# A decoder on one core: the maximum pass of cross attention in four tiles, and newer self attention and last experts

## The reference

```python
x = x + L0_attn(layernorm(x))                     # 16 heads of 64
x = x + L0_xattn(ctx_1024, layernorm(x))          # ("context mixing")
x = x + L0_ffn(layernorm(x));  x = x + L1_attn(layernorm(x))
x = x + L1_xattn(layernorm(x), ctx_1024, ctx_1024)    # the same in layers 2 and 3
# cross attention of layers 1 to 3, 16 heads of 8:
#   Q, K, V = projections;  scores = Q K^T * scale
#   attn = softmax(scores);  out = (attn V) Wo + bo
...
x = x + L3_ffn(layernorm(x))
# 32 experts take at most 70 tokens each, 16 adapters shared by pairs:
#   idx = argsort(-score)[:cap];  out = scatter_add(w * expert(x[idx]))
```

## Time and profile before

| what | us |
|---|---|
| median of three runs (4217.76 to 4238.39) | 4232.51 |
| the profiled execution | 4240.81 |
| its span, first to last instruction | 4239.0 |
| PE busy | 3631.5 (86%) |
| DVE busy | 2559.1 (60%) |
| ACT busy | 2099.3 (50%) |
| POOL busy | 1553.1 (37%) |
| mean granted clock of TensorE | 0.929 |

### The profile page before, as it was taken

How to read it: one execution, slowest core, us unless ns; L and a number is a source line. 1 busy time by engine, 2 the same in 40 slices (tenths; PEclk the granted TensorE clock), 3 DMA queues, 4 the chain that set the end, 5 groups by cost and what they waited for, 6 DMA issues and landing times. The chain is left out here.

```text
span 4239.0 us, 113125 instructions
## 1 busy us (share of the span) xinstructions
PE 3631.5 (86%) x48174; PEld 2493.0 (59%) x48174; DVE 2559.1 (60%) x4447; ACT 2099.3 (50%) x2832; POOL 1553.1 (37%) x1827
## 2 busy tenths in 40 slices
PE   7976459999997887799999988978899999983698
PEld 5654227777775445477777754434477777761475
DVE  4522568877774445578777753345578777756543
ACT  3344437766664232267666652344376666651010
POOL 1100037667661000267667620012476676620000
PEclk9998779999998899999999988988899999995798
DMA  4062045655651430356655621100356556520575
GB/s 147 2 252 104 2 108 148 151 145 147 156 140 37 97 85 4 93 140 151 154 141 149 156 50 55 54 7 8 85 138 155 149 140 159 150 57 1 141 194 130
DMA packets 203247, 464.39 MB, mean 110 GB/s; under 512 B 87486, under 2 KB 94398, under 8 KB 202590
## 3 DMA queue, kind: packets, MB, share of 16 engines
q1 hardware_dynamic: 200622, 455.30, 41.4%
q10 hardware_dynamic: 2160, 2.29, 0.2%
HBM read 212.72 MB, written 1.72 MB: 51 GB/s over the span
## 5 line engine op out<-in xcount | busy, mean ns | idle before, releaser
L1435 DVE TENSOR_REDUCE x_bank_top<-ps 112x1 f32<-112x500 f32 x2304 | 1419.2, 672 | 469.8 <-PE ps L1151 463.3
L1287 ACT ACTIVATE x_probs_t<-ps 128x1344 f32<-128x1344 f32 x768 | 991.8, 1291 | 211.3 <-PE ps L1168 206.8
L1168 PEld LDWEIGHTS ps<-x_queries,x_keys 128*128 128x128 bf16 x9216 | 488.1, 98 | 330.4 <-issue 150.3
L1151 PE MATMUL ps<-x_keys,x_queries 96*112 96x500 bf16 x2304 | 633.8, 381 | 24.7 <-DMA x_keys<-x_key_part 15.2
L1168 PE MATMUL ps<-x_queries,x_keys 128*128 128x112 bf16 x9216 | 584.2, 213 | 38.8 <-ACT x_probs_t L1287 36.6
L1181 PE MATMUL ps<-x_probs_t,x_values 128*32 128x112 f32 x18432 | 490.5, 263 | 5.5 <-ACT x_probs_t L1287 4.1
L1181 PEld LDWEIGHTS ps<-x_probs_t,x_values 128*32 128x32 f32 x18432 | 443.3, 111 | 70.2 <-issue 65.2
L1368 POOL TENSOR_TENSOR x_key_part<-x_key_whole,x_nothing 128x500 bf16<-128x500 f32 x270 | 337.2, 1249 | 255.9 <-ACT x_key_whole L1272 255.9
L1372 POOL TENSOR_TENSOR x_key_part<-x_key_left,x_nothing 128x500 bf16<-128x500 f32 x270 | 340.4, 1261 | 21.2
L1139 PE MATMUL ps<-x_wv,x_ctx_t 128*128 128x128 f32 (+1 forms) x2304 | 329.3, 286 | 10.4 <-issue 10.4
L1151 PEld LDWEIGHTS ps<-x_keys,x_queries 96*112 96x112 bf16 x2304 | 258.9, 131 | 128.0 <-DVE x_bank_top L1435 37.1
(11 more groups left out here) (455 smaller groups left out, 4521.8 us busy)
## 6 DMA issues: line engine op xcount, KB each, us to landing
x_keys<-x_key_part SPq DMA_DIRECT2D x1143, 192.0 KB, 3.7
x_ctx_t<-in_ctx_t SPq DMA_DIRECT2D x96, 750.0 KB, 6.1
cm_ctx_n<-in_ctx_n SPq DMA_DIRECT2D x32, 768.0 KB, 6.0
cm_ctx_t<-in_ctx_t SPq DMA_DIRECT2D x32, 750.0 KB, 8.3
e_share<-m_weight_scratch SPq DMA_DIRECT2D x32, 490.0 KB
e_spread_out<-m_slot_scratch SPq DMA_DIRECT2D x32, 490.0 KB
x_queries<-x_query_part SPq DMA_DIRECT2D x558, 28.0 KB, 2.7
e_share<-m_weight_rows SPq DMA_DIRECT2D x32, 448.0 KB, 6.1
```

The source lines that it names most:

```text
L1151: nc.tensor.matmul(ps[0:RW, n, 0:KB], queries[i // 2 % 2][0:TALL, p, i % 2, :], keys[i % 2][0:TALL, p, KB * n:KB * n + KB], start=True, st ...
L1168: mm = nc.tensor.matmul(ps[:, TURNED + c // VC, RW * (c % VC):RW * (c % VC) + RW], keys[i % 2][:, p, KT * c:KT * c + KT], queries[i // 2 % ...
L1287: nc.scalar.activation(probs_t[PROBS[p]].rearrange("k (n c) r -> k n (c r)", c=VC), ps[:, TURNED:TURNED + VR, 0:VC * RW], ACT.Exp, scale=s ...
L1435: nc.vector.tensor_reduce(bank_top[0:RW, p, n:n + 1], ps[0:RW, n, 0:KB], AX_X, ALU.max).then_inc(topped, 1)
```

## The change

In cross attention the maximum pass goes by single heads. The slots lie in the rows 16 to 111, so that each head of a pair lies in one half of the 128 rows; a call does four matmuls of 64 rows and 64 columns, for two pairs (column halves) and two heads (row halves), into two banks: 12 calls an item in place of 24 matmuls. The rows for the maxima are now 0 to 15 and 112 to 127; ACT alone places the maxima, and POOL clears them again for a later item. A call stands before and one after values or keys in a step, and one between two halves of each mix. Self attention normalises inside its block, has three load semaphores, two mix buffers, and makes its scores two pairs ahead, behind the mix. The last experts have a ring of three buffers, no loops, loads of rows ahead of weights, and gather from three bf16 parts of the tokens, which ACT and POOL split beside the router.

```diff
@@ self_attention_0
+        norm = Norm(chip, x, xn, True, squares, roots, (4, 5, 6, 7))
...
-            for n in range(-1, NP_):
+            for n in range(-2, NP_):
                 if n >= 0:
                     turn(n)
-                if n + 1 < NP_:
-                    make_scores(n + 1)
-                if n > 0 and n % 2 == 0:
-                    project_out(n // 2 - 1)
                 for g, t in halves(n):
                     project(g, t)
                 if n >= 0:
                     mix_values(n)
-                if n + 1 < NP_:
+                if n + 2 < NP_:
+                    make_scores(n + 2)
+                if 0 <= n + 1 < NP_:
                     make_values(n + 1)
+                if n > 0 and n % 2 == 0:
+                    project_out(n // 2 - 1)
...
         @block.scalar
...
                 for g, t in halves(n):
                     if t % 4 < 2:
                         keep_made(g, t)
-                if n + 1 < NP_:
-                    exponentials(n + 1)
+                if 0 <= n + 1 < NP_:
                     keep_values(n + 1)
+                if n + 2 < NP_:
+                    exponentials(n + 2)
...
@@ cross_attention
-            def scores(i, p):
...
-                for n in range(NB_):
-                    wait(pe, topped, NB_ * (PR * i + p - 1) + n + 1)
-                    nc.tensor.matmul(ps[0:RW, n, 0:KB], queries[i // 2 % 2][0:TALL, p, i % 2, :], keys[i % 2][0:TALL, p, KB * n:KB * n + KB],
-                                     start=True, stop=True).then_inc(scores_done, 1)
+            def scores(i, m, n):
...
+                unit = UNITS * (HP_ * i + m) + 2 * n
+                for c in range(2):
+                    for r in range(2):
+                        if c == 0:
+                            wait(pe, topped, unit + r - 2)
+                        p, rows = 2 * m + c, slice(64 * r, 64 * r + 64)
+                        mm = nc.tensor.matmul(ps[64 * c:64 * c + 64, (unit + r) % NB_, 0:KB], queries[i // 2 % 2][rows, p, i % 2, r, :],
+                                              keys[i % 2][rows, p, KB * n:KB * n + KB], start=True, stop=True)
+                        if c == 1:
+                            mm.then_inc(scores_done, 1)
...
             def turn_tops(i, h):
...
-                nc.tensor.matmul(ps[TALL:P, MIX, 2 * RW:3 * RW], top_parts[:], ident_low[:, 0:RW], start=True, stop=True).then_inc(tops_turned, 1)
+                for r in range(2):
+                    mm = nc.tensor.matmul(ps[0:TOPS, MIX, 2 * RW + P * r:2 * RW + P * r + P], top_parts[:, r, :], ident_low[:], start=True, stop=True)
+                mm.then_inc(tops_turned, 1)
...
+                    ahead, pair = divmod(step + LEAD, PR)
+                    if has(i + ahead) and pair % 2 == 0 and step % HP_ != 1:
+                        scores(i + ahead, pair // 2, 0)
                     if step in VALUE_STEPS and has(i + 1):
                         make_values(i + 1, VALUE_STEPS.index(step))
                     if step == FOLD_STEP and has(i - 1):
                         fold(i - 1)
-                    ahead, pair = divmod(step + LEAD, PR)
-                    if has(i + ahead):
-                        scores(i + ahead, pair)
+                    if has(i + ahead) and pair % 2 == 1:
+                        scores(i + ahead, pair // 2, 2)
                     if step in KEY_STEPS and has(i + 3):
                         make_keys(i + 3, KEY_STEPS.index(step))
-                    if step == 0 and has(i - 1):
-                        mix_values(i - 1, 1)
-                    if step == HP_ and has(i):
-                        mix_values(i, 0)
+                    if has(i + ahead) and pair % 2 == 0:
+                        scores(i + ahead, pair // 2, 1)
+                    for part in range(2):
+                        if step == 0 and has(i - 1):
+                            mix_values(i - 1, 1, part)
+                        if step == HP_ and has(i):
+                            mix_values(i, 0, part)
+                        if step % HP_ == 0 and part == 0:
+                            ahead, pair = divmod(step + 1 + LEAD, PR)
+                            if has(i + ahead):
+                                scores(i + ahead, pair // 2, 0)
...
+            def place_tops(i, h):
+                act.wait_ge(tops_turned, 2 * i + h + 1)
+                for r in range(2):
+                    turned = ps[0:TOPS, MIX, 2 * RW + P * r:2 * RW + P * r + P].rearrange("k (c s) -> k c s", c=2)[:, :, 0:S]
+                    last_copy = nc.scalar.copy(of_batch(i)[0:TOPS, HP_ * h:HP_ * h + HP_, r].rearrange("k (m c) s -> k m c s", c=2), spread(turned, 1, 2))
+                last_copy.then_inc(tops_placed, 1)
...
                     if has(i):
                         exponentials(i, step)
+                    if step == 2 and has(i):
+                        place_tops(i, 1)
+                    if step == 6 and has(i + 1):
+                        place_tops(i + 1, 0)
...
+            for part in query_parts:
+                nc.gpsimd.memset(part[:, :, :, S:], 0.0).then_inc(zeros_ready, 1)
...
-                    nc.vector.tensor_reduce(bank_top[0:RW, p, n:n + 1], ps[0:RW, n, 0:KB], AX_X, ALU.max).then_inc(topped, 1)
...
+                    nc.vector.tensor_reduce(bank_top[:, m, r, n:n + 1], ps[:, unit % NB_, 0:KB], AX_X, ALU.max).then_inc(topped, 1)
...
@@ experts_by_slot
-    PAIRS, SUBS, LOADS = 16, 2, 6
+    PAIRS, SUBS, LOADS, DEEP = 16, 2, 6, 3
...
+            for n in range(PAIRS):
+                u = n % DEEP
+                if n >= DEEP:
+                    sp.wait_ge(used[u], n // DEEP)
...
-                    mm = nc.tensor.matmul(ps[:, gather_bank(u), 0:2 * CAP], by_token[:, t, :], marks[u][:, t].rearrange("p e k -> p (e k)"),
-                                          start=(t == 0), stop=(t == NP_ - 1))
+                    for k in range(PARTS):
+                        mm = nc.tensor.matmul(ps[:, gather_bank(n), 0:2 * CAP], token_parts[k][:, t, :], marks[n % 2][:, t].rearrange("p e k -> p (e k)"),
+                                              start=(t == 0 and k == 0), stop=(t == NP_ - 1 and k == PARTS - 1))
```

323 lines of the change are left out of this document (183 added, 140 removed).

## The result

The change makes the kernel slower by half a per cent. Median of 19 runs 4257.24 us (4229.74 to 4309.42) against 4236.43 us for the kernel before (19 runs, 4217.76 to 4245.44); ratio 1.0051, 95% interval 1.0036 to 1.0066, so +15 to +28 us. I had forecast 4192, -40 us. The time lies inside the range, but the sign is wrong.

A forecast was written before the change was run, and what follows sets the result against it. PE was taken as the bound of the cross attentions, the bulk of the time. Cross attention +14 and +4, self attention -18 and experts -40 summed to -40 us against the median 4232.5: 4192, range 4115 to 4275.

The forecast's parts named there:

- The steady pass: Cross attention, one pass on PE from one L1157 to the next: 22.45 us, against 22.29 before.
- the terms of a quad: Cross attention: four small matmuls at once take 0.23 us with their starts; each change of tile shape 0.13.
- My own stretches, 13.6 and 8.87: Parts of a cross-attention pass: 13.6 us from L1168 of step 5 to L1157, set by POOL; 8.87 the rest, PE's own.
- POOL's wait ahead of L1214: End of a pass's first stretch: PE would still wait there for POOL, whose chain takes 13.6 us against PE's 13.5.
- At each stage's start ... 1.5 x 3 = +4 us: Cross-attention stage starts: POOL clears three more pads, 0.5 us each, and ACT waits; +4 us over three stages.
- +0.15, times 96: Cross attention: each of 96 passes grows by 0.15 us, +14 us in all.
- My slower rival: Cross attention: shape changes cost more, 0.8 us a pass, +80 us, 4270; slower from +0.6 a pass; chance 0.17.
- Its 4390: Severe form of the slower case: row halves do not overlap, a quad takes 0.43 us, +2 us a pass.
- Self attention: forecast -18: Earlier weight loads -8.7 us, scores two ahead 3 of 11 us kept and 6 at the end; between -12 and -26.
- "Their rate is bounded by that 13.2 us": Last experts: with three buffers loads run without a gap, 13.2 us a set; steps of 13.6, -32 us over 15.
- the third rival: Little gain: loads hold experts at 14.5 us a step, self attention gives only its head; 4214 to 4225; chance 0.2.
- The 8 us for the last step: Last experts: the last step's 3.17 us on DVE's path and the low clock go, -8 us.

The follow-up runs named there:

- rows_split: Kernel before, each load of 32 rows into partitions 96 to 127 issued as two of 16 neighbouring partitions; ratio 1.0051 (1.0031 to 1.0071), +22 us.
- rows_strided: Kernel before, each load of 32 rows issued as two of 16, the even and the odd partitions of 96 to 127; ratio 0.9996 (0.9975 to 1.0016).
- changed_again: The changed kernel unaltered, run and profiled once more on another chip; ratio to the kernel before 1.0073 (1.0047 to 1.0099).

## Why the prediction was wrong

- The steady pass was right: 22.43 us against 22.45, in both stretches, and with it the terms of a quad: 0.21 us for itself (I had 0.23 with its starts) and 0.09 to 0.13 for a change of shape. (My own stretches, 13.6 and 8.87, add up to 22.47; the slip is 2 us in the whole.) One reading of it was not: POOL's wait ahead of L1214 is gone. PE's own first stretch is 13.65 us where I had 13.5, and POOL is done with the maxima 0.18 us before it ends.
- "At each stage's start ... 1.5 x 3 = +4 us" failed, and it is the step that turned the sign. The pads cost nothing that can be seen. The loads of the pair rows, which the diff splits and moves, delay the first fill by 12 us a stage, 35 in all, and I had priced them at nothing without giving a reason. I had looked at the passes and not at the start of a stage. rows_split and rows_strided show the cause of 7 of the 12: sixteen neighbouring partitions a load where there were thirty-two.
- "+0.15, times 96" took every pass as steady. Of the 6.4 us in 29 passes some 4 are the 0.14 of a steady pass; the rest lies in single passes of 22.8 to 25 us, of which the kernel before has some too. The two passes ahead of the last, in which no keys are made any more and PE waits for ACT in some steps, took 2.4 us more.
- The cross attention was thus forecast at +18 and measured at +57 (43 to 70), 39 us of the 61 by which the whole was missed; the experts are another 22. My slower rival had the right sign and the wrong place: it asked for 0.6 us in every pass. (Its 4390 fits +2 us a pass alone; on top of the 0.8 it would have been near 4460.)
- Self attention: forecast -18, measured -22 (14 to 30), the stage 16 to 17 us shorter. The sum was right, its parts less so: the start gave 10.8 us where I had 8.7, all that follows some 6 where I had 9. That they cancel is luck.
- Experts: forecast -40, measured -18 (10 to 27). PE's step of 13.3 was right. "Their rate is bounded by that 13.2 us" failed: it was the time of one set on engines that were free between sets. Back to back 3.0 MB took 15 us at 198 GB/s, and the steps averaged 14.5. This is the third rival, "held by the loads at 14.5 us a step", to which I gave 0.2. The 8 us for the last step failed too: L1952 takes 12.28 us in changed_again as before. It goes with the clock of the execution and not with the change: the same step takes 12.3 us in 6 of the 10 profiles with the old experts and in 3 of the 10 with the new, and 6.2 or 6.3 in the others.

What stays open: the other 5 us at the first fill, the long single passes, and why the clock stays low for up to 23 us behind the first fill in some starts of the new cross attention and for 4 in others.

## To carry to other kernels

Price the bookkeeping of a layout change, its constants and zeros, like its arithmetic: which partitions a load covers decided 7 us here, three times over. A load time read between gaps is no rate, and a rate divided by its share of busy time is none either: 184 GB/s at 0.71 became 198 at 0.90. And where another engine bounds the end of a stage, work that keeps PE's clock up, even idle work, can be worth more than the change itself (-16 us here, between -8 and -25).

## What the runs showed of the hardware

- Packets of 24 KB took 3.0 us each on average where a load covered 16 neighbouring partitions (rows_split), and 2.0 us where it covered 32, or 16 spread over 32 (before, rows_strided).
- A change of PE's tile shape costs 0.09 us in the instruction ahead of a quad (L1222 0.68 to 0.70 us instead of 0.60) and 0.13 in the quad itself, before bf16 weights and before float32 ones.
- The same packets of 1536 bytes took 66 ns in the kernel before, with the DMA engines busy for 0.71 of the experts, and 115 ns in changed_again, at 0.90: what a third set in flight fills is paid for in longer packets.
- Behind the first fill of a stage TensorE's clock stayed at its lower level for 3 to 23 us, differently in starts of the same kernel, and each such stretch lengthened the way to the first exponential, from 16 or 17 us up to 23.
